# Moving a transpose, two bias loads and one tile's normalisation from the start of the FFN into self-attention's last group, and adding the FFN's results two tiles at a time

## The reference, cut to what matters

```python
x = x + xattn(layernorm(x), ctx_1024, ...)
x = x + self_attn(layernorm(x), wq, wk, wv, wo)      # 16 heads of 64, causal
x = x + ffn(layernorm(x))

def ffn(x):                                          # W_in 256 x 1024, W_out 1024 x 256
    W_in_q  = round(W_in  * 127 / amax_per_column) / scale
    W_out_q = round(W_out * 127 / amax_per_row) / scale
    x_q     = round(x * 32767 / max|x|) / scale      # one scale over all 2048 tokens
    hidden  = gelu(x_q @ W_in_q + b_in)
    h_q     = round(hidden * 32767 / max|hidden|) / scale
    return h_q @ W_out_q + b_out
```

## Time and profile before

| | |
|---|---|
| time, median of 3 runs | 651.74 us (651.53 to 652.11) |
| profiled execution: its own time | 651.54 us |
| its span, first to last instruction | 649.7 us |
| mean granted TensorE clock | 0.989 of full speed |
| self-attention's last quad | 537.2 to 560.4 us of the span |
| FFN front, up to the first `hidden` matmul | 560.7 to 573.6 us |
| FFN `hidden` and the second maximum | 573.6 to 609.7 us |
| FFN second half, with the last store | 609.7 to 649.7 us |

### The profile page before, as it was taken

How to read it: one execution, slowest core, us unless ns; L and a number is a source line. 1 busy time by engine, 2 the same in 40 slices (tenths; PEclk the granted TensorE clock), 3 DMA queues, 4 the chain that set the end, 5 groups by cost and what they waited for, 6 DMA issues and landing times. The chain is left out here.

```text
span 649.7 us, 18558 instructions
## 1 busy us (share of the span) xinstructions
PE 602.3 (93%) x6777; PEld 515.6 (79%) x6777; DVE 470.7 (72%) x989; ACT 386.3 (59%) x1016; POOL 155.4 (24%) x219
## 2 busy tenths in 40 slices
PE   6599999999999999889889999999999998699997
PEld 3598888888888898758777979797979797444597
DVE  4478788888888888667899665757575657367797
ACT  3488788888888888755333333333333334257795
POOL 6524243424343423000301212112121203060000
PEclk9799999999999999999999999999999999999999
DMA  6996767676777767804000000000000000000012
GB/s 202 266 259 174 188 158 183 169 191 169 183 175 182 174 163 204 256 15 130 3 2 2 2 0 0 0 0 0 0 0 0 3 2 2 10 0 2 0 49 82
DMA packets 37036, 58.43 MB, mean 90 GB/s; under 512 B 6912, under 2 KB 15232, under 8 KB 36992
## 3 DMA queue, kind: packets, MB, share of 16 engines
q1 hardware_dynamic: 29328, 42.75, 25.7%
q10 hardware_dynamic: 4592, 8.78, 4.7%
q0 software_dynamic: 3072, 6.30, 4.0%
HBM read 17.96 MB, written 2.10 MB: 31 GB/s over the span
## 5 line engine op out<-in xcount | busy, mean ns | idle before, releaser
L617 ACT ACTIVATE Pr<-pS,nmax 128x256 f32<-128x256 f32 x256 | 120.0, 484 | 26.9 <-DVE nmax L725 26.8
L725 DVE TENSOR_REDUCE nmax<-pS 128x2 f32<-128x512 f32 x128 | 87.3, 684 | 21.7 <-PE pS L461 20.1
L471 PE MATMUL pT<-ident,Pr 128*128 128x128 f32 x512 | 78.6, 276 | 3.2 <-DVE wraw L730 3.1
L953 POOL TENSOR_TENSOR a_Pr<-a_Pr,a_rinv 128x512 f32<-128x512 f32 x32 | 32.8, 1045 | 185.8 <-DVE a_rinv L1242 185.8
L461 PE MATMUL pS<-Kst,Qst 96*128 96x256 f32 x256 | 58.9, 313 | 12.4 <-DMA Qst<-QSl 6.9
L1122 ACT ACTIVATE a_Pr<-a_Pr 128x512 f32<-128x512 f32 x32 | 20.2, 631 | 76.0 <-DVE a_Pr L1234 76.0
L471 PEld LDWEIGHTS pT<-ident,Pr 128*128 128x128 f32 x512 | 60.0, 142 | 4.5 <-issue 4.2
L461 PEld LDWEIGHTS pS<-Kst,Qst 96*128 96x128 f32 x256 | 40.3, 194 | 21.1 <-issue 9.1
L617 ACT ACTIVATION_READ_ACCUMULATOR Pr<-pS,nmax 128x1 f32 x256 | 55.1, 215 | 0.0
L280 POOL DMA_DIRECT2D Qst<-QSh x60 | 30.2, 506 | 80.8 <-PE pS L461 56.2
L59 PE MATMUL a_pJ<-a_XTh,a_W1h 128*128 128x256 f32 x128 | 37.1, 290 | 2.5 <-DVE X L1255 1.6
(11 more groups left out here) (316 smaller groups left out, 1972.9 us busy)
## 6 DMA issues: line engine op xcount, KB each, us to landing
Kst<-WO_ints SPq DMA_DIRECT2D x96, 128.0 KB, 3.3
CT<-ctxT ACTq DMA_DIRECT2D x16, 512.0 KB, 4.9
Kst<-KSh SPq DMA_DIRECT2D x62, 128.0 KB, 2.7
Qst<-QSh SPq DMA_DIRECT2D x64, 64.0 KB, 2.4
Qst<-QSh POOLq DMA_DIRECT2D x64, 64.0 KB, 3.0
Kst<-KSl SPq DMA_DIRECT2D x31, 128.0 KB, 3.2
Qst<-QSl SPq DMA_DIRECT2D x32, 64.0 KB, 2.3
Qst<-QSl POOLq DMA_DIRECT2D x32, 64.0 KB, 2.9
```

Source lines behind the costliest of these rows:

```text
L471: last = pe.transpose(pT[s % 2][:, t, k, :], Pr[s % 2][:, t, P * k:P * k + P], ident[:, :])
L617: act.activation(Pr[c % 2][:, t, :], pS[c % 2][:, t, :], ACT.Exp, bias=nmax[c % 2][:, t:t + 1], accum_out=rsum[par][:, c // 4, 2 * (c % 4) ...
L725: dve.tensor_reduce(nmax[s % 2][:, :], pS[s % 2][:, :, :], AX.X, ALU.max, negate=True).then_inc(maxed, 1)
L953: pool.tensor_tensor(rows, rows, rinv[s][:, :].unsqueeze(2).to_broadcast([P, 8, SQ]), ALU.mult).then_inc(weighted, 1)
```

## The change

It moves work in three places and changes the order of work in two.

1. `bias_in`, `bias_out` and the transposed `W_in` get storage that outlives the blocks (`ffn.hold`). SP issues both bias loads in self-attention's block, right behind the loads of the two FFN weights.
2. The last quad has an order of its own on PE, `LAST`. It has two new steps `I`, each with eight transposes of `W_in` into a `pJ` bank, and ACT copies each out (`turned_w_in`). `weigh 1` now stands ahead of `Y 0`.
3. Within the last quad, DVE (with POOL) normalises tile 14 between the additions of `Y 0` and `Y 1`; the FFN block is left with tile 15 alone.
4. In the FFN front the transposes of `W_in` go; `keep_busy` is called with 12 and, behind the spread, with 5 (it was 8, 3 and 6). `hidden` waits for each half of the split input on its own.
5. In the second half `add_rows` handles two tiles of one PSUM bank in one instruction, behind the low parts of `f` = 1 and 3. `tile_done` is counted up by four when a whole group is multiplied. In the last group PE leaves `f` = 6 and 7 to the end and does them first for tiles 0 and 1 and then for tiles 2 and 3.

```diff
@@ self_attention
+        LAST = [("score", 0), ("V", 0), ("V", 1), ("score", 1), ("V", 2), ("V", 3), ("I", 0), ("turn", 0), ("turn", 1),
+                ("I", 1), ("weigh", 0), ("turn", 2), ("turn", 3), ("weigh", 1), ("Y", 0), ("Y", 1)]
...
@@ sync
+            sp.dma_start(ffn.bias_in[:, :], b_in).then_inc(bias_loaded[0], 16)
+            sp.dma_start(ffn.bias_out[:, :], b_out.partition_broadcast(P)).then_inc(bias_loaded[1], 16)
@@ gpsimd
+                if last:
+                    pool.wait_ge(l3_mv, TILES - 1)
+                    pool.tensor_scalar(vare3[:, 0:1], mv3[:, 0, 1:2], LN_EPS, None, ALU.add).then_inc(l3_ve, 1)
+                    pool.wait_ge(l3_ve, QUADS)
+                    pool.tensor_tensor(rstd3[:, 0:1], vare3[:, 0:1], half[:, 0:1], ALU.pow).then_inc(l3_rs, 1)
@@ tensor
+                elif kind == "I":
+                    pe.wait_ge(ints_made, 1)
+                    for f in range(FK):
+                        last = pe.transpose(out[:, :].bitcast(BF16)[:, P * f:P * f + P],
+                                            ffn.WI[:, f, P * part:P * part + P], identb[:, :])
@@ scalar
+            def turned_w_in(r, part, bank):
+                act.wait_ge(proj, r + 1)
+                act.activation(ffn.turned[:, part, :], pJ[bank][:, :].bitcast(BF16), ACT.Copy).then_inc(w_in_turned, 1)
...
+                if last:
+                    fills("I", 0)
                 copy_turned(i, 0)
                 copy_turned(i, 1)
+                if last:
+                    fills("I", 1)
@@ vector
-                fills("Y", 0)
+                if not last:
+                    fills("Y", 0)
                 o_low(i, 2)
                 o_low(i, 3)
...
+                if last:
+                    fills("Y", 0)
+                    dve.wait_ge(x_done, TILES - 1)
+                    dve.bn_stats(stats3[:, 0, :], X[:, TILES - 2, :]).then_inc(l3_st, 1)
+                    dve.wait_ge(l3_st, TILES - 1)
+                    dve.bn_aggr(mv3[:, 0, :], stats3[:, 0, :]).then_inc(l3_mv, 1)
+                    dve.wait_ge(l3_rs, QUADS)
+                    dve.tensor_scalar(ffn.XN[:, TILES - 2, :], X[:, TILES - 2, :], mv3[:, 0, 0:1], rstd3[:, 0:1],
+                                      ALU.subtract, ALU.mult).then_inc(l3_xn, 1)
+                    dve.wait_ge(l3_xn, TILES - 1)
+                    dve.tensor_reduce(ffn.x_tile_max[:, QUADS - 1:QUADS], ffn.XN[:, TILES - 2, :], AX.X,
+                                      ALU.max, apply_absolute_value=True)
                 fills("Y", 1)
@@ feed_forward
-            for k in range(KC):
-                for f in range(FK):
-                    last = pe.transpose(bankb[:, P * f:P * f + P], ffn.WI[:, f, P * k:P * k + P], identb[:, :])
-                last.then_inc(w_turned, 1)
-                keep_busy(pe, 8 if k == 0 else 3, bank[0][:, :], identb, causal)
-                pe.wait_ge(w_copied, k + 1)
+            keep_busy(pe, 12, bank[0][:, :], identb, causal)
...
             spread_max(0)
-            keep_busy(pe, 6, bank[0][:, :], identb, causal)
+            keep_busy(pe, 5, bank[0][:, :], identb, causal)
...
             def hidden(g, last):
-                pe.wait_ge(x_lo, 2 * g + 2)
...
+                        if f == 0:
+                            pe.wait_ge(x_lo, 2 * g + k + 1)
...
+            def multiply(g, f, tiles):
+                pe.wait_ge(g_lo, FK * g + f + 1)
+                for t in tiles:
+                    for s in (HI, LO):
+                        m = pe.matmul(out_tile(g, t), GT_[f % RING][s][:, P * t:P * t + P], ffn.WO[:, f, :],
+                                      start=(f == 0 and s == HI and t % 2 == 0), stop=(f == FK - 1 and s == LO),
+                                      skip_group_check=True)
+                return m
+
+            LATE = FK - 2
             for g in range(GROUPS):
                 after(pe, y_done, GT * (g - 1))
...
+                final = g == GROUPS - 1
+                for f in range(LATE if final else FK - 1):
+                    multiply(g, f, range(GT)).then_inc(second, 1)
+                if not final:
+                    multiply(g, FK - 1, range(GT)).then_inc(tile_done, GT)
+            for pair in ((0, 1), (2, 3)):
+                for f in range(LATE, FK):
+                    last = multiply(GROUPS - 1, f, pair)
+                last.then_inc(tile_done, 2)
...
+            def add_rows(g, pair):
+                dve.wait_ge(tile_done, GT * g + 2 * pair + 2)
+                t = GT * g + 2 * pair
+                rows = X[:, t:t + 2, :].rearrange("p a d -> p (a d)")
+                dve.scalar_tensor_tensor(rows, bank[2 * (g % 2) + pair][:, :], a_step[1][:, 0:1], rows,
+                                         ALU.mult, ALU.add).then_inc(y_done, 2)
...
-                    if g and 1 <= f <= GT:
-                        add_rows(g - 1, f - 1)
+                    if g and f in (1, 3):
+                        add_rows(g - 1, f // 2)
```

More of the change, by code:

```diff
@@ L90, in build @@
             w_step=keep("w_step", [P, 2, FF // P], F32),
-            x_tile_max=keep("x_tile_max", [P, QUADS], F32),
+            x_tile_max=keep("x_tile_max", [P, QUADS + 1], F32),
             XN=XN3)
+        bias_loaded = [whole.enter_context(nc.semaphore(f"bias_loaded_{n}")) for n in ("in", "out")]
         raw_in = [whole.enter_context(nc.semaphore(f"raw_in{m}")) for m in range(4)]
@@ L95, in build @@
                         raw, raw_in, ffn.WO, (awq, awk, awv, awo))
-        self_attention(nc, X, ident, identb, causal, half, raw, raw_in, ffn, w_inT, w_out)
-        feed_forward(nc, X, ident, identb, causal, half, ffn, b_in, b_out, out)
+        ffn.hold(keep("WI", [P, KC, FF], BF16), keep("bias_in", [P, FF // P], F32), keep("bias_out", [P, D], F32))
+        self_attention(nc, X, ident, identb, causal, half, raw, raw_in, ffn, w_inT, w_out,
+                       b_in, b_out, bias_loaded)
+        feed_forward(nc, X, ident, identb, causal, half, ffn, bias_loaded, out)
 class Ffn:
@@ L106, in __init__, with hold @@
         self.XN, self.x_tile_max = tensors["XN"], tensors["x_tile_max"]
+    def hold(self, turned, bias_in, bias_out):
+        self.turned, self.bias_in, self.bias_out = turned, bias_in, bias_out
 def statistics_of(dve, stats, mv, X, quad, stats_done, mv_done, waited):
@@ L825, in _, with self_attention @@
             add_rows(PAIRS - 1)
-def self_attention(nc, X, ident, identb, causal, half, raw, raw_in, ffn, w_inT, w_out):
+def self_attention(nc, X, ident, identb, causal, half, raw, raw_in, ffn, w_inT, w_out, b_in, b_out, bias_loaded):
     EV = 16
@@ L905, in self_attention @@
                 ("K", 2), ("K", 3), ("Y", 1)]
+        LAST = [("score", 0), ("V", 0), ("V", 1), ("score", 1), ("V", 2), ("V", 3), ("I", 0), ("turn", 0), ("turn", 1),
+                ("I", 1), ("weigh", 0), ("turn", 2), ("turn", 3), ("weigh", 1), ("Y", 0), ("Y", 1)]
         def plan(last):
             k, work = 0, []
-            for kind, s in PLAN:
+            for kind, s in LAST if last else PLAN:
                 if kind in ("score", "turn", "weigh"):
                     work.append((kind, s, None))
-                elif not (last and kind in ("X", "Q", "K")):
+                else:
                     work.append((kind, s, k))
@@ L979, in bank_read @@
                     pe.wait_ge(x_done, 2 * quad + part + 1)
+                elif kind == "I":
+                    pe.wait_ge(w_in_turned, part + 1)
                 else:
@@ L1078, in body @@
                     else:
-                        quad = i if kind in "VY" else i + 1
+                        quad = i if kind in "VYI" else i + 1
                         bank_read(*held[k % 2])
@@ L1143, in _ @@
                     copy(r, kind, part, r % 2, None)
+            def turned_w_in(r, part, bank):
+                act.wait_ge(proj, r + 1)
+                act.activation(ffn.turned[:, part, :], pJ[bank][:, :].bitcast(BF16), ACT.Copy).then_inc(w_in_turned, 1)
             def body(i, last):
                 def fills(kind, part):
-                    if kind == "V" or not last:
+                    if kind in "VI" or not last:
                         k = place(kind, part, last)
-                        if kind == "X":
+                        if kind == "I":
+                            turned_w_in(EV0 + EV * i + k, part, k % 2)
+                        elif kind == "X":
                             x_high(EV0 + EV * i + k, part, k % 2)
@@ L1361, in body, with feed_forward @@
                     round_w(1)
+                if last:
[10 more added lines that the diff above has]
+                                      ALU.max, apply_absolute_value=True)
                 fills("Y", 1)
             steps(dve, body)
-def feed_forward(nc, X, ident, identb, causal, half, ffn, b_in, b_out, out):
+def feed_forward(nc, X, ident, identb, causal, half, ffn, bias_loaded, out):
     G = 512
@@ L1382, in feed_forward @@
         table = sb("table", [P, 1], F32)
```

(28 more changed lines are left out.)

18 lines of the change are left out of this document (4 added, 14 removed).

## The result

The changed kernel took 646.94 us (median of 5 runs, 646.47 to 648.61) against 651.53 for the kernel before (5 runs): a ratio of 0.9933, with a 95% interval of 0.9918 to 0.9948. The forecast was 646.3, between 645.2 and 648.4. The profiled execution took 646.78, its span is 644.8, 4.9 less than before. The kernel before spreads more: on the chip of e5 to e7 its 20 runs took 648.62 to 654.88, with a mean granted clock of 0.989 to 0.991 in the five shortest and 0.984 to 0.987 in the five longest, so what one execution gains can lie well off the 4.6 of the medians.

What follows compares the result with a forecast made beforehand. TensorE is busy 93% of a 649.7 us span, so time is won where it idles or does unread work. Terms -0.6 - 5.1 + 0.3 = -5.4 give 646.1 against the profile, 646.3 against the median; range 645.2 to 648.4.

Steps and rivals of the forecast that it cites:

- Part 1: Self-attention's last quad: new order and tile 14's earlier normalisation gain 0.6 us, bounds 0 to 0.8.
- Part 2: The FFN's front: first `hidden` matmul about 7.7 us after PE's start, before 12.85; gain 5.1, bounds 2.5 to 5.5.
- The clock rival: FFN front: the granted clock halves there too, giving 1.3 to 2.6 us back; time 647.6 to 648.9, chance 0.13.
- `hidden` itself is paced by PE and moves as a block: FFN's `hidden` stage: paced by PE at 0.216 us a matmul, its length forecast to change by 0.
- Part 3: The FFN's second half, with paired additions: a loss of 0.3 us, bounds a loss of 1.0 and a gain of 0.7.
- The tail: End of the second half: 4.95 us from PE's start on `f` = 4 in place of 5.4, gain 0.45.
- Group 1: Second half: 0.15 us lost, as two paired additions stand ahead of `f` = 4 instead of three single ones.
- the loop: Second half, PE and DVE waiting in turn: a group takes 8.4 us where it took 8.06, closing twice, 0.6 lost.
- The rule of the Trainium skill's page "VectorE: DVE Perf Modes": Second half's paired additions: one large tile pays the fixed cost once, an estimated gain of some 0.13 us a pair.
- The rival built on the rule: Second half: the wait on `tile_done` is covered and pairs simply pay, -0.6 us there; time 645.4, chance 0.11.

Runs made afterwards that it cites:

- e5: Changed kernel without the twelve `keep_busy` matmuls at the start of the FFN block: 648.36 us, ratio 0.9955.
- e7: Changed kernel with tile 14 normalised together with tile 15 in the FFN block again, `keep_busy` still 12: 648.02 us, ratio 0.9955.
- e6: Changed kernel with `Y 0` ahead of `weigh 1` again in the last quad: 648.06 us, ratio 0.9944.
- e1: Kernel before, with only the two bias loads moved into self-attention, behind the FFN weight loads: 648.08 us, ratio 0.9948.
- e10: Changed kernel with tile 14 normalised in the FFN block again and 16 `keep_busy` matmuls at its start in place of 12: 647.47 us, ratio 0.9931.
- e4: Changed kernel with POOL's additions of `b_out` to `X` started only when the last group's input is split: 645.72 us, ratio 0.9913.
- e3: Changed kernel with `tile_done` counted up by two behind each pair of tiles in groups 0 to 2, paired additions kept: 645.84 us, ratio 0.9912.
- e2: Changed kernel with single additions, `tile_done` for each tile and the old order in the last group: 645.91 us, ratio 0.9916.

## Why the prediction was right, point by point

- **Part 1** came out as worked: 0.65 for 0.6. ACT's new copies delayed `weigh 0` by 0.9 and the second copies by 0.2 (0.4 forecast), each counted from the quad's start, and tile 14's reduction (559.10, 0.42) ended beside `Y 1`'s result. What the prediction did not price alone is the order, 1.37 by e6; without it part 1 would have been a loss.
- **Part 2**: 5.25 for 5.1. The maximum was found 2.78 after the block's start (2.85 forecast), the turn began at 5.37 (5.3), and `keep_busy` decided the start of `hidden` at 7.60 (7.6 to 7.7). By e1, e7 and e10 the 5.25 divide into 3.3 for the load (taken out of the kernel before), 1.0 for the tile (put back into the changed one), and 0.9 left for the transposes of W_in and the rest; no run moves the transposes alone. The clock rival named its condition rightly, gaps on PE: e5 shows its price, 2.5.
- **The step that failed** is "`hidden` itself is paced by PE and moves as a block". It lost 0.45. PE starts `hidden` on the first half of the split input, 0.45 ahead of where it stood in the old kernel relative to POOL's start (POOL waits for the second half). But the rounding of group 2 ends 0.55 after POOL's last addition, in both kernels, so the head start was lost there. e4 shows it: without the overlap 0.62 come back, the 0.45 and about the 0.2 that the overlap had already cost the kernel before (0.94 in place of 0.74). The Trainium skill's page "SBUF — State Buffer", in "Who interferes with whom", says that VectorE shares its second pair of ports with GpSimd, that `tensor_scalar` is one of the operations that can take this pair, and that whoever issues first has it for the whole instruction while the other is blocked; the trace agrees, with 0.74 alone, 0.94 and 1.36 beside POOL. It fits the other way round too: POOL's first addition, which begins at 568.25 while DVE still rounds group 1 (568.08 to 568.82), takes 2.81 and the other three 2.36; in e4, where no rounding runs beside them, all four take 2.36.
- **Part 3**: right in place and sign, under-sized: a loss of 0.47 for 0.3. The tail came as forecast: 4.95 from PE's last start on `f` = 4 to the end of the last addition (642.26 - 637.31), against 5.40. Group 1 came 0.15 late, as forecast. The term that was mis-sized is the loop: groups are 8.45 apart where 8.06 stood, so it costs 0.78 over its two turns, not 0.6. Nearly half of that miss is the sum itself: the prediction's own 8.4 against 8.06 gives 0.68 for two turns.
- **The rule of the Trainium skill's page "VectorE: DVE Perf Modes"** holds as a price: 0.66 for a pair, 0.80 for two. As a gain of time it is not shown. e3, where the pair no longer waits for the whole group, has a second half 0.18 shorter than before and 0.19 shorter than e2's, but this is the tail's 0.45 less 0.15 in group 1 and 0.13 over the two turns (8.12 against 8.06). The rival built on the rule had the saving on DVE right. The coarse count took away 0.65, and without it ACT and DVE wait for each other, so that the saving still does not shorten a group. How the tail's 0.45 divides between the pairing and the new order of the last group was not separated.

## What to carry to other kernels

When two small instructions become one, look at what the larger one has to wait for: the 0.13 saved on each pair came with a wait that cost 0.65, because its semaphore was counted once for four tiles; two lines took that back. Look also at which other engines are as full as the one that is relieved: the saving on DVE did not shorten the groups, since ACT was at 8.0 a group itself (e3). When work is moved out of a stage, `keep_busy` cover must be made to fit the gap that is left: twelve matmuls fit the change; with one tile more they were too few, and that cost 1.2. And when a stage is started earlier, ask what in it is timed by another engine; here it was a bias addition on POOL, which does not appear in the chain of waits there.

## What the runs showed of the hardware that was not expected

An instruction blocked by another engine shows in the profile as busy, not as waiting: DVE's rounding stands there as 1.36 of work in place of 0.75, with no releaser, and only its end, 0.55 behind the end of POOL's, tells why. And a load of 4 KB took 3.49 us from issue to use, as long as sixteen matmuls of 512 columns at full clock; by e1 it cost more (3.3, over a third of it through the clock) than the tile, the transposes and the last quad's gain together (1.0 + 0.9 + 0.65).
